# A gated graph network on one core: the lower half of each state is made by VectorE at the end of the next step instead of by GpSimd

## The reference

```python
h = jnp.maximum(_layernorm(x, axis=-1), 0.0)
A = (adj != 0).astype(x.dtype)
for l in range(weight.shape[0]):                  # 5
    m = jnp.einsum('bnd,de->bne', h, weight[l])
    agg = jnp.einsum('bij,bid->bjd', A, m)
    h = _gru_cell(agg, h, w_ih, w_hh, b_ih, b_hh)
x = x + h * mask[..., None]
...
def _gru_cell(m, h, w_ih, w_hh, b_ih, b_hh):
    gi = m @ w_ih.T + b_ih
    gh = h @ w_hh.T + b_hh
    i_r, i_z, i_n = jnp.split(gi, 3, axis=-1)
    h_r, h_z, h_n = jnp.split(gh, 3, axis=-1)
    r = jax.nn.sigmoid(i_r + h_r)
    z = jax.nn.sigmoid(i_z + h_z)
    n = jnp.tanh(i_n + r * h_n)
    return (1.0 - z) * n + z * h
```

## Time and profile before

| | |
|---|---|
| median of 3 runs | 747.81 us (746.2 to 748.32) |
| profiled execution | 748.27 us, its span 746.4 us |
| mean granted TensorE clock | 0.995 |
| TensorE busy | 686.7 us, 92% |
| VectorE busy | 562.7 us, 75% |
| ScalarE busy | 539.2 us, 72% |
| GpSimd busy | 300.7 us, 40% |
| DMA | 21.10 MB, mean 28 GB/s |
| `rh` rows, the steps | 80, beginning 29.2 to 664.5 us |

### The profile page before, as it was taken

How to read it: one execution, slowest core, us unless ns; L and a number is a source line. 1 busy time by engine, 2 the same in 40 slices (tenths; PEclk the granted TensorE clock), 3 DMA queues, 4 the chain that set the end, 5 groups by cost and what they waited for, 6 DMA issues and landing times.

```text
span 746.4 us, 12659 instructions
## 1 busy us (share of the span) xinstructions
PE 686.7 (92%) x4226; PEld 589.6 (79%) x4226; DVE 562.7 (75%) x1398; ACT 539.2 (72%) x1131; POOL 300.7 (40%) x427
## 2 busy tenths in 40 slices
PE   3899899989999989989999999989999999988896
PEld 2688678878888779878888778878888888877666
DVE  4688986888867976788977876798876787776344
ACT  5577778668878877668878878657888677657543
POOL 4322525463244343564234434473333234643412
PEclk9999999999999999999999999999999999999999
DMA  6520011200000020410000020110000000110001
GB/s 159 137 66 1 2 29 31 57 1 4 6 4 1 1 61 1 139 32 4 6 4 1 2 60 1 58 58 2 6 6 1 2 1 0 57 58 7 6 1 58
DMA packets 47624, 21.10 MB, mean 28 GB/s; under 512 B 9032, under 2 KB 47560, under 8 KB 47560
## 3 DMA queue, kind: packets, MB, share of 16 engines
q1 hardware_dynamic: 47560, 20.29, 10.1%
HBM read 15.27 MB, written 4.19 MB: 26 GB/s over the span
## 4 chain that ended last, share of the span: by engine, by line
PE 49%; DVE 22%; ACT 13%; POOL 8%; issue 7%; DMA 1%; DVEq 0%; SPq 0%; POOLq 0%; ACTq 0%
PE bank L404 8%; PE bank L406 8%; PE bank L405 8%; PE bank L399 6%; DVE rh L1341 3%; DVE zh L1317 3%; POOL rstd L926 2%; ACT xn L704 2%; DVE hd L1325 2%; PE bank L390 2%; PE bank L592 2%; PE bank L604 2%; PE bank L607 2%; PE bank L542 2%; POOL dis L970 2%
## 5 line engine op out<-in xcount | busy, mean ns | idle before, releaser
L942 POOL TENSOR_TENSOR h_lo<-h,h_hi 128x512 fp32r<-128x512 f32 x64 | 84.3, 1317 | 255.2 <-ACT h_hi L875 255.2
L1341 DVE SCALAR_TENSOR_TENSOR rh<-bank,rh 128x512 f32<-128x512 f32 x80 | 55.1, 689 | 91.4 <-ACT bank L892 91.3
L404 PE MATMUL bank<-h_hi,whh_hi 128*128 128x512 f32 x240 | 105.8, 441 | 12.2 <-DVE rh L1341 11.5
L404 PE MATMUL bank<-g_hi,wc_hi 128*128 128x512 f32 x240 | 102.4, 427 | 0.0
L406 PE MATMUL bank<-h_lo,whh_hi 128*128 128x512 f32 x240 | 95.3, 397 | 0.0
L405 PE MATMUL bank<-h_hi,whh_lo 128*128 128x512 f32 x240 | 94.9, 395 | 0.0
L406 PE MATMUL bank<-g_lo,wc_hi 128*128 128x512 f32 x240 | 94.3, 393 | 0.0
L405 PE MATMUL bank<-g_hi,wc_lo 128*128 128x512 f32 x240 | 93.7, 390 | 0.0
L399 PEld LDWEIGHTS bank<-edge,hn 128*128 128x128 f32 x640 | 84.0, 192 | 9.5 <-DVE edge L1042 3.1
L399 PE MATMUL bank<-edge,hn 128*128 128x128 f32 x640 | 84.8, 276 | 2.9 <-DVE edge L1042 2.9
L704 ACT ACTIVATE xn<-x_res,shift,rstd 128x128 f32<-128x128 f32 x128 | 55.4, 484 | 31.2 <-POOL shift L928 31.2
(11 more groups left out here) (168 smaller groups left out, 1659.2 us busy)
## 6 DMA issues: line engine op xcount, KB each, us to landing
x_in<-in_x SPq DMA_DIRECT2D x8, 512.0 KB, 5.4
adj_in<-in_adj SPq DMA_DIRECT2D x8, 512.0 KB, 4.9
x_res<-in_x SPq DMA_DIRECT2D x16, 256.0 KB, 2.8
out_x<-x_res SPq DMA_DIRECT2D x16, 256.0 KB, 2.3
xz<-x_res SPq DMA_DIRECT2D x16, 50.0 KB
w_sb<-in_L_gnn_W SPq DMA_DIRECT2D x1, 640.0 KB, 5.4
w_sb<-in_L_gnn_W SPq DMA_DIRECT2D x5, 128.0 KB, 5.3
rows<-in_adj SPq DMA_DIRECT2D x32, 0.6 KB
```

The source lines that it names most:

```text
L404: nc.tensor.matmul(dst[:], w_hi, m_hi, start=start, stop=False)
L942: nc.gpsimd.tensor_tensor(h_lo[q][:], h[q][:], h_hi[q][:].bitcast(f32), ALU.subtract).then_inc(sem["h_lo_new"], 1)
L1341: nc.vector.scalar_tensor_tensor(rh[:], R_BANK[:], 1.0, rh[:], ALU.add, ALU.mult).then_inc(sem["rh_ready"], 1)
```

## The change

`low_half` moves from GpSimd's block into VectorE's: the same subtraction with the same wait for the upper half and the same semaphore for TensorE. GpSimd called it at the head of step n for the state n - 1. VectorE calls it in step n for the state n - 1 too, but behind `new_state(n)` and ahead of `beside(2n+1)`.

```diff
--- before.py
+++ after.py
@@ in the block of GpSimd
-            def low_half(n):
-
-                q = n % QUADS
-                pool.wait_ge(sem["h_hi_new"], n // STEPS * SPLITS + n % STEPS + 1)
-                nc.gpsimd.tensor_tensor(h_lo[q][:], h[q][:], h_hi[q][:].bitcast(f32), ALU.subtract).then_inc(sem["h_lo_new"], 1)
-
...
             for n in range(ALL + TAIL_STEPS):
-                if n and n <= ALL and (n - 1) % STEPS < SPLITS:
-                    low_half(n - 1)
                 beside(2 * n)
                 beside(2 * n + 1)
@@ in the block of VectorE
+            def low_half(n):
+
+                q = n % QUADS
+                dve.wait_ge(sem["h_hi_new"], n // STEPS * SPLITS + n % STEPS + 1)
+                nc.vector.tensor_tensor(h_lo[q][:], h[q][:], h_hi[q][:].bitcast(f32), ALU.subtract).then_inc(sem["h_lo_new"], 1)
+
...
                 kept_state(n)
                 new_state(n)
+                if n and (n - 1) % STEPS < SPLITS:
+                    low_half(n - 1)
                 beside(2 * n + 1)
```

## The result

The changed kernel takes 757.96 us (median of 4 runs, 757.62 to 759.16), the kernel before on the same chip 747.0 us (4 runs, 746.12 to 748.32). The ratio is 1.0152, with a 95% interval of 1.0134 to 1.0171: slower by 1.5%. The forecast was 757.0, and as a difference 9.3 us, where the medians differ by 11.0. The profiled execution took 758.3 us with a span of 756.5 and a mean granted clock of 0.990 (before: 748.27, 746.4, 0.995).

A forecast was written before the change was run, and what follows sets the result against it. No one engine bounds it: the chain lies on TensorE 49%, VectorE 22%, ScalarE 13%. Added 18.6 less released 6.6 and 2.7 makes 9.3 us, on 748.27 giving 757.6, less 0.46 for the median: 757 us, range 752 to 762.

The forecast's parts named there:

- The lower half's own date: TensorE's state product reads it three steps after GpSimd makes it, some 20 us; one step later wins or loses nothing.
- The added term: VectorE's 64 new subtractions behind `h`, 0.60 us each, 38.4 in all, of which 18.6 us lie on the path.
- the 23 that I took as full: Steps where VectorE's added subtraction was to lengthen the path by its whole 0.60 us, such as 6 to 9.
- twelve partial ones: Steps in rounds 1 to 3, four each, where the added 0.60 us is partly covered; 0.4 us taken for each.
- The hidden 29: Remaining insertions, covered by VectorE's wait for the r gate's tanh (L892) before `rh`; 17.4 us more if uncovered.
- The released term: GpSimd no longer holding VectorE's `ones_r`, `mix`, `deg_some` gives back 6.6 us; its earlier adjacency scaling gives 2.7 more.
- The 2.7: GpSimd's scaling L982, some 2 us earlier, misses VectorE's `zh` and two `h`: 1.35 us in each of rounds 1 and 2.
- Holds that come back: Rival: GpSimd holds the new subtraction or other VectorE instructions instead; 762 to 766 us, chance 0.13.
- Ties: Rival: TensorE nearly as late as VectorE, so partial steps and 8 full ones cost nothing; 746 to 750 us, chance 0.15.
- Faster: Rival: GpSimd's holds on VectorE give back 9.3 us while additions land in idle time; 741 to 745 us, chance 0.10.
- The clock: Rival: grown TensorE waits make its granted clock fall, about 1.7 us each; 765 us and more, chance 0.03.
- The rule: Rival: whole-instruction port lock lets GpSimd's 128x4 power operation hold `deg_some` about 0.4 us in three rounds; 758.3 us, chance 0.04.

The follow-up runs named there:

- the one without the lower half: Kernel before with GpSimd's lower-half subtraction removed after a round's first states and nothing added to VectorE; TensorE reuses the first states' halves: 737.72 us, ratio 0.988.
- 747.23: Kernel before with only 29 of the 64 lower halves, those predicted as hidden, moved to VectorE, the other 35 staying on GpSimd: 747.23 us, ratio 0.9997.
- the 35 alone: Kernel before with only the 35 lower halves predicted as costing time moved to VectorE, the other 29 staying on GpSimd: 761.73 us, ratio 1.0188.

## Why the prediction was right

**The lower half's own date costs nothing.** No wait of TensorE in the changed kernel is put down to `h_lo`.

**The added term, 18.6 us.** By the difference of the changed kernel and the one without the lower half it is 20.2, by the steps 20.9. The 0.60 us of one is right to 0.01 (88.25 to 88.85). Step by step against that kernel, 19 of the 23 that I took as full cost 0.59 to 0.62 (27 and 47 among them, under the release of L982's hold); 32 and 52 cost only 0.25 and 0.27, 29 and 49 0.32. Of the twelve partial ones, at 0.4 each, eight (23, 43, 63, 28, 48, 31, 51, 68) cost 0.57 to 0.68, and 26, 46, 66 and 69 0.41 to 0.53. The listed steps come to 19.4 in place of 18.6, and step 10, where the clock stayed down longer, adds 1.1. The partial ones, 6.7 in place of 4.8, are what was sized too low; the full ones, 12.7 in place of 13.8, were a little too high.

**The hidden 29.** Near right as a sum: about 1 us and not nothing. That 747.23 shows none of it is luck, since `ones_r`, released with them, gave as much back. They hide by slack one or two steps later, and twice the added work shows how thin it was.

**The released term, 6.6 and 2.7.** Measured 9.27 together, 8.7 by the steps, and `ones_r`, `mix` and `deg_some` came back to what I gave. The 2.7 was too high: steps 27 and 28, with 0.80 and 0.26, gave what `zh` and the first `h` were worth, but step 29 gave 0.96 where `deg_some` and the second `h` should give 1.28, and 49 alike. Steps 10 and 11 gave 0.5 that I had not counted, with a granted clock of 0.68 in 94 to 98 and not 0.57. Round 3 gave 1.0 and not 1.7, for two reasons. Step 60 gave only 0.53 when its `mix` was released, because in the kernel without the lower half the granted clock fell just ahead of it; in the kernel of the 35 alone, whose trace has no such fall, steps 20, 40 and 60 give 0.97 alike. With the pass ahead of `rh`, whose trace has such a fall ahead of both, steps 40 and 60 give 0.55 and 0.56. The fall in the kernel without the lower half:

```profile
488.00:492.00 4.00, 3.41 (x12) 2.77 (x13) 3.93 (x10) 2.85 (x6) 3.86 (x3) 0.63 0.21 62
```

The kernel before has 1.00 at this place, and TensorE's wait for `rh` ahead of it is the same in both (1.34 and 1.35 us). What brings this fall about stays open; in the changed kernel it comes in step 39 instead. And step 70 takes back 0.39 of the 0.81 that step 69 gives. It does so in each kernel in which GpSimd doesn't make the lower half of step 69's state, and in no other; which wait comes to light in it I have not followed.

**Where the two errors went.** By the steps the added term was 2.3 too low and the released one 0.6 too high, both in the same direction, so the difference was 12.2 and not 9.3. Of that error the medians show 1.7, and the forecast time is nearer still only because the kernel before ran lower. The mechanism and the sign were right; the last microsecond was luck.

**The rivals.** *Holds that come back*: they did, in steps 12 and 76 (`h` and `h_lo` at 1.61 and 1.52, and at 1.35 and 1.52 us), where there was room, so that they cost next to nothing net: step 76 is 1.25 longer than before and step 77 1.06 shorter. Nothing in the argument had put them there; with the 35 alone, one of 0.97 us lies on the path three times. *Ties*: of the 23 only four were absorbed in part. *Faster* needed all the partial ones and 11 of the 23 full ones hidden. *The clock*: one longer stretch, in steps 10 and 11, 0.5 us, and one more, in step 39, 0.4 us. Neither lies behind a wait of TensorE that had grown, as the rival had it: 3.84 us for 4.28 ahead of the first, 1.36 for 1.35 ahead of the second. *The rule*, by which the 128x4 power operation would hold `deg_some`: here are VectorE and GpSimd in round 2 of the changed kernel.

```profile
425.61 0.17 DVE L1059 TENSOR_SCALAR deg_some<-deg 128x9 f32<-128x9 f32 x1
```

```profile
425.07 1.01 POOL L926 TENSOR_TENSOR rstd<-var_eps,neg_half 128x4 f32<-128x4 f32 x1
```

The two meet, as the rule's case had it, and `deg_some` takes its undisturbed 0.17. The small power operation held nothing.

## What to carry to other kernels

When an operation goes from one engine to another, its price is not its duration: count the steps that have no wait behind the new place, and on the giving side the holds that its long instructions put on others. Put added work right ahead of the engine's own wait: the same 64 passes cost 20 us behind `h` and 9 ahead of `rh`. Where one large GpSimd instruction stands alone, holds VectorE, and GpSimd has time to spare, cut it in four before moving it; here that gave 3.9 us. Where GpSimd is itself on the path, the cut costs more than the hold, and where it makes many cut instructions without a pause, VectorE can be shut out through several of them (2.3 us at worst here).

## What was not expected of the hardware

- A hold can hang on 0.03 us. A `mix` that begins 0.03 us ahead of GpSimd's instruction takes 0.69, and GpSimd's takes 1.80 for 1.28; a `mix` that begins 0.59 behind takes 1.65. So parts of a change don't add up while the large instructions are there (7.5 us over the sum) and do once they are short (0.9 us under it).
- Cutting 128x512 into four of 128x128 costs GpSimd 0.42 us for the subtraction (1.28 to 1.70) and 0.43 for the scaling by a broadcast column (1.04 to 1.47); with one quarter held by VectorE the scaling is 1.92.
- Short instructions don't always end a hold: one of VectorE's was held through seven of GpSimd's in a row, 2.99 us for 0.68.
- A wait of TensorE grown from 1.24 to 1.85 us, beside less work in the steps around it, came with a fall of the granted clock to 0.59 in the next 4 us, 1.6 us of time. What in it brings the fall about was not tried apart.
- `ones_r`, 128x128, took 1.19 us against a large GpSimd instruction and 0.20 alone: a small VectorE instruction loses as much as a large one.
